# Three score banks, two first-pass banks, and a half unit made ahead of the context matmuls

## What is computed

```python
x = x + attn(layernorm(x))
    # content = einsum('bqhd,bkhd->bhqk', q + u_bias, k)
    # pos     = rel_shift(einsum('bqhd,khd->bhqk', q + v_bias, p))
    # attn    = softmax((content + pos) / sqrt(128));  ctx = attn @ v @ Wo
x = x + ffn(layernorm(x))
    # router: Wr1, layernorm, gelu, Wr2, softmax, top 2
    # y = (x1 * gelu(x2)) @ W2[e], weighted and added for the two experts
```

## Time and profile before

| what | value |
|---|---|
| median of 3 runs | 1681.2 us (1679.35 to 1681.27) |
| the profiled execution | 1680.72 us |
| its span, first to last instruction | 1679.0 us |
| attention loop, in the span | 88 to 1234 us |
| expert phase, in the span | about 1310 us to the end |

### The profile page before, as it was taken

One profiled execution on the slowest core, in us unless ns is written; L12 is line 12 of the kernel. 1 busy time (PEld: TensorE's weight loads), 2 busy tenths in 40 slices (PEclk: granted clock), 3 DMA queues, 4 the chain that ended last, 5 costly groups with the idle time before them and its releaser, 6 DMA issues. The chain is left out here.

```text
span 1679.0 us, 50905 instructions
## 1 busy us (share of the span) xinstructions
PE 1548.0 (92%) x12492; PEld 1204.6 (72%) x12493; DVE 1397.8 (83%) x5262; ACT 1108.9 (66%) x2295; POOL 1103.0 (66%) x2088
## 2 busy tenths in 40 slices
PE   3789999999999999999999999999952699999997
PEld 1567776677777767777777776776741699999997
DVE  4669899989989987998998899899864588887886
ACT  2157777776777776677777777767730477777775
POOL 5247767767766775777677677667673276666665
PEclk8679999999999998999999999999985799999999
DMA  5746535535644553464365355346454244444443
GB/s 136 198 116 174 148 93 152 164 96 128 180 116 128 161 148 84 110 203 110 104 174 148 93 141 164 97 129 179 122 153 136 42 58 54 56 56 52 56 53 49
DMA packets 133844, 199.72 MB, mean 119 GB/s; under 512 B 20888, under 2 KB 95016, under 8 KB 133632
## 3 DMA queue, kind: packets, MB, share of 16 engines
q1 hardware_dynamic: 108064, 177.07, 39.0%
q0 software_dynamic: 25568, 20.14, 8.2%
HBM read 108.10 MB, written 75.20 MB: 109 GB/s over the span
## 5 line engine op out<-in xcount | busy, mean ns | idle before, releaser
L1084 DVE CUSTOM_DVE_ANT_0 junk<-pA,lmask 128x512 bf16<-128x512 f32 x1056 | 686.9, 683 | 65.1 <-PE pA L671 45.9
L986 ACT ACTIVATE prob<-pB 128x512 f32<-128x512 f32 x384 | 229.8, 598 | 205.5 <-PE pB L690 115.9
L1578 POOL DMA_INDIRECT out<-yb,dst x142 | 230.4, 1622 | 131.3 <-ACT yb L1656 78.5
L692 PE MATMUL pB<-QL,K 97*128 97x512 f32 (+3 forms) x768 | 286.4, 373 | 1.4 <-ACT upper_diag L986 1.2
L669 PE MATMUL pA<-K,QL 96*128 96x512 f32 (+3 forms) x792 | 282.1, 357 | 5.1 <-DMA K<-split_operands 3.4
L690 PE MATMUL pB<-QU,K 97*128 97x512 f32 (+3 forms) x640 | 267.5, 418 | 0.2
L671 PE MATMUL pA<-K,QU 96*128 96x512 f32 (+3 forms) x660 | 233.1, 354 | 4.4 <-DVE acc L1084 3.2
L988 ACT ACTIVATE prob<-pB 128x512 f32<-128x512 f32 x384 | 227.9, 594 | 12.7 <-PE pB L692 3.4
L708 PE MATMUL pC<-prob,vext 128*17 128x256 f32 x3088 | 217.8, 385 | 0.1
L576 POOL TENSOR_TENSOR prob<-prob,upper_diag 128x128 f32<-128x128 f32 x384 | 179.7, 468 | 31.9
L690 PEld LDWEIGHTS pB<-QU,K 97*128 97x128 f32 x640 | 122.0, 191 | 99.9 <-issue 62.3
(11 more groups left out here) (305 smaller groups left out, 3642.9 us busy)
## 6 DMA issues: line engine op xcount, KB each, us to landing
QL<-split_operands SPq DMA_DIRECT2D x67, 256.0 KB
QU<-split_operands SPq DMA_DIRECT2D x67, 256.0 KB
K<-split_operands SPq DMA_DIRECT2D x67, 256.0 KB
xg<-routed_rows SPq DMA_DIRECT2D x75, 132.0 KB
split_operands<-c_h SPq DMA_DIRECT2D x36, 256.0 KB, 6.1
split_operands<-c_l SPq DMA_DIRECT2D x36, 256.0 KB, 6.4
QL<-split_operands SPq DMA_DIRECT2D x67, 128.0 KB
QU<-split_operands SPq DMA_DIRECT2D x67, 128.0 KB
```

What stands on the lines that cost most here:

```text
L692: mm = pe.matmul(pB[:, q0 + up:q0 + HALF], K[0:r, s, k], QL[0:r, s, q0 + up:q0 + HALF], start=True, stop=True)
L986: act.activation(p[:, 0:HALF], pB[:, 0:HALF], ACT.Exp, scale=SCALE).then_inc(p_exp, 1)
L1084: v.tensor_tensor_reduce(out, src[:, :], lmask[:, at:at + HALF], 1.0, -3.0e38, ALU.add, ALU.max, acc[:, s, qb, n % 2:n % 2 + 1]).then_inc( ...
L1578: po.indirect_dma_start(dram["out"], bass.IndirectOffsetOnAxis(dst[k][:, a:a + 1], 0), yb[k][:, a, :], None, compute_op=ALU.add).then_inc( ...
```

## The change

`pB` becomes three tensors of one bank each (`S2_BUFS = 3`), and `S1_BUFS` goes from 3 to 2. Half units are counted through, g = 2 x unit + half, and half g goes into `pB[g % 3]`; it waits until the exponential of half g-3 has been taken. A chunk waits until VectorE has read chunk n-2. At the places where contexts follow a unit (u = 1, 4, 6, 8), the first half of the next unit is issued before the contexts and no longer after them and the small work. Before and after the loop the third extra bank is `pB[2]` and no longer `pA[2]`. Line numbers shift by 2 to 6.

```diff
-S1_BUFS = 3
+S1_BUFS = 2
+S2_BUFS = 3
...
-        pB, pC = pb("pB", [P, S]), pb("pC", [P, S // STRIPS])
+        pB, pC = [pb(f"pB{i}", [P, HALF]) for i in range(S2_BUFS)], pb("pC", [P, S // STRIPS])
+        outside = (*pA, pB[2])
...
             def project(nb, j, part=0, parts=1):
-                dst = (pE, *pA)[j % 4] if first else pE
+                dst = (pE, *outside)[j % 4] if first else pE
...
             def second_pass(b, h, u, half):
-                pe.wait_ge(p_exp, HPB * (b * (H * S2U) + h * S2U + u) + half + 1)
-                r, q0 = MROW + 1, HALF * half
+                g = HPB * (h * S2U + u) + half
+                pe.wait_ge(p_exp, HPB * (b * (H * S2U)) + max(g, 1))
+                r, q0, dst = MROW + 1, HALF * half, pB[g % S2_BUFS]
...
-                        mm = pe.matmul(pB[:, q0:q0 + up], K[0:r, s, k], QU[0:r, s, q0:q0 + up], start=True, stop=True)
+                        mm = pe.matmul(dst[:, 0:up], K[0:r, s, k], QU[0:r, s, q0:q0 + up], start=True, stop=True)
...
                     for u in range(S2U):
-                        second_pass(b, h, u, 0)
+                        if (h, u) == (0, 0) or (u - 1) % S2U not in PAIRS_AT:
+                            second_pass(b, h, u, 0)
                         first_pass(b, h + AHEAD, 2 * u)
                         second_pass(b, h, u, 1)
                         first_pass(b, h + AHEAD, 2 * u + 1)
                         if u in PAIRS_AT:
+                            if (h, u) != (H - 1, S2U - 1):
+                                second_pass(b, h + (u + 1) // S2U, (u + 1) % S2U, 0)
                             back, kb = PAIRS_AT[u]
                             context(b, h + back, kb)
...
             pe.wait_ge(s1_read, (B * H + AHEAD) * S1U)
+            pe.wait_ge(p_exp, HPB * (B * H * S2U + 1))
             for j in range(2):
                 pe.wait_ge(m_done, m_at(B, f"turn {j}") + 1)
-                project_out(j, pA[1 + j]).then_inc(w_ready, 1)
-            pe.wait_ge(p_exp, HPB * (B * H * S2U + 1))
+                project_out(j, outside[1 + j]).then_inc(w_ready, 1)
...
-                        act.activation(p[:, 0:HALF], pB[:, 0:HALF], ACT.Exp, scale=SCALE).then_inc(p_exp, 1)
+                        act.activation(p[:, 0:HALF], pB[HPB * n % S2_BUFS][:, :], ACT.Exp, scale=SCALE).then_inc(p_exp, 1)
                         act.wait_ge(s2_ready, HPB * (b * (H * S2U) + n) + 3)
-                        act.activation(p[:, HALF:S], pB[:, HALF:S], ACT.Exp, scale=SCALE).then_inc(p_exp, 1)
+                        act.activation(p[:, HALF:S], pB[(HPB * n + 1) % S2_BUFS][:, :], ACT.Exp, scale=SCALE).then_inc(p_exp, 1)
```

More of the change, by code:

```diff
@@ L689, in second_pass @@
                     if up > 0:
-                        mm = pe.matmul(pB[:, q0:q0 + up], K[0:r, s, k], QU[0:r, s, q0:q0 + up], start=True, stop=True)
+                        mm = pe.matmul(dst[:, 0:up], K[0:r, s, k], QU[0:r, s, q0:q0 + up], start=True, stop=True)
                     if up < HALF:
-                        mm = pe.matmul(pB[:, q0 + up:q0 + HALF], K[0:r, s, k], QL[0:r, s, q0 + up:q0 + HALF], start=True, stop=True)
+                        mm = pe.matmul(dst[:, up:HALF], K[0:r, s, k], QL[0:r, s, q0 + up:q0 + HALF], start=True, stop=True)
                 else:
@@ L695, in second_pass @@
                         k = slice(k0, k0 + P)
-                        mm = pe.matmul(pB[:, k], K[0:r, s, k], QU[0:r, s, k], start=True, stop=True)
+                        mm = pe.matmul(dst[:, k0 - q0:k0 - q0 + P], K[0:r, s, k], QU[0:r, s, k], start=True, stop=True)
                 mm.then_inc(s2_ready, 1)
@@ L870, in _ @@
             pe.wait_ge(m_done, m_at(B, "rows 1") + 1)
[L871 to L874, removed]
+            router_hidden(range(NB), outside[1]).then_inc(m_ready, 1)
+            router_fold(B, outside[2]).then_inc(m_ready, 1)
+            router_logits(B, pB[0]).then_inc(m_ready, 1)
+            router_ranks(B, pB[1]).then_inc(m_ready, 1)
         @block.scalar
@@ L887, in evacuate @@
                 half = slice(HALF * (j % 2), HALF * (j % 2) + HALF)
-                src = (pE, *pA)[j % 4] if isinstance(nb, int) and nb == 0 else pE
+                src = (pE, *outside)[j % 4] if isinstance(nb, int) and nb == 0 else pE
                 if j < 2:
@@ L1037, in _ @@
                 copied(f"rows {j}", (pE, pA[0])[j], m_done)
-            fold(B, pA[2])
+            fold(B, outside[2])
             tanh(B)
@@ L1370, in _ @@
                 v.wait_ge(w_ready, B * W_N + 1 + j)
-                final(j, pA[1 + j], w_done)
+                final(j, outside[1 + j], w_done)
                 router_stats(B, range(4 * j, 4 * j + 4))
@@ L1375, in _ @@
             v.wait_ge(m_ready, m_at(B, "hidden") + 1)
-            router_bias(B, pA[1])
+            router_bias(B, outside[1])
             hidden_stats(B)
@@ L1382, in _ @@
             v.wait_ge(m_ready, m_at(B, "logits") + 1)
-            logits_out(pB[:, 0:HALF])
+            logits_out(pB[0])
             for part in range(4):
@@ L1386, in _ @@
             v.wait_ge(m_ready, m_at(B, "ranks") + 1)
-            places(B, 0, pB[:, HALF:S])
+            places(B, 0, pB[1])
             for part in (1, 2):
```

## The result

The changed kernel takes 1728.0 us (median; 1726.7 to 1732.3) against 1681.2 us (a fourth run of the kernel before took 1690.4 and leaves that median as it is): ratio 1.027, interval 1.023 to 1.031. It is slower by 47 us; 40 were forecast (1721, range 1698 to 1746).

The account below looks back on a forecast made before the run. TensorE was taken to bound the loop through its start-to-start times. From the profiled 1680.7 us, 40 - 2.6 - 1 + 0 + 4 = +40.4 gave 1721 us, range 1698 to 1746.

Parts of the forecast that it names:

- Part 1: Attention loop: chunks wait longer with two chunk banks, 40 us in eight turns, less 2.6 for a vanished router-row wait.
- the six places: Loop, (head step, unit): (0, 8), (1, 4), (2, 1), (3, 3), (4, 3), (4, 8), with delays of 0.31 to 0.97 us.
- (1, 4): Head step 1, unit 4 of the loop: chunk delayed 0.87 us, of which 0.19 vanishes in an existing wait, leaving 0.68.
- (5, 1): Head step 5, unit 1: a further 0.3 us delay, left out because TensorE waits behind it for VectorE's router work anyway.
- Part 2: Attention loop: three score banks shorten TensorE's waits for exponentials, a gain of 1 us, ends 0 and 8.
- Part 3: Attention loop: issuing the next unit's first half ahead of the contexts is worth 0, with 2 us either way.
- Part 4: Outside the loop: 34 chunks ahead of it cost 1 to 7 us more with two banks, taken as +4 us.
- What would show it: Signs in the trace after: turn 146 to 147 us, VectorE idle 5 us more, head steps 2 and 3 lengthened most.
- a sign against the bank wait: Loop: the bank wait is not the cause if head steps 1 to 4 do not lengthen more than 5 to 7.
- The clock: Rival: more TensorE waiting puts three or four more loop turns at the low clock, to 1750 us; chance 0.14.
- Absorbed: Rival: TensorE has slack in the loop that makes up part of the 5 us a turn, 1683 to 1706; chance 0.14.
- Faster: Rival: the score bank was the loop's true shortage, so the gain passes the cost, 1666 us; chance 0.06.

Follow-up runs that it names:

- the run with six waits: Kernel before, with only the chunks at (0, 8), (1, 4), (2, 1), (3, 3), (4, 3) and (4, 8) in the loop waiting for chunk n-2: 1703.6 us, ratio 1.014.

## Why the prediction was right, and where it was not

**What bounds the kernel.** TensorE, through its start-to-start times: right. One wait more for every chunk lengthens the turn by 4.9 us with nothing else changed. The rule on the busy share of weight loads (the Trainium skill, "Perfetto Trace Analysis", Identifying the Most-Contended Engine) would have had TensorE at 71% with slack to absorb it. The weight loads' share still reads 69% (100.8 of 146.26), and the loss was paid almost in full. The measurement decides for start-to-start times here.

**Part 1, 40 us less 2.6.** The loop lost 37.6. The delays at the six places are right to 0.02 us each when they stand alone, and the sum is right by errors that cancel, which is luck. In the run with the wait in the loop alone, the steps up add to 6.3 us a turn and the steps down to 1.6. The prediction had about 5.2 and 0.5.

The steps up. The six places, each with the chunks that lead up to it, give 3.6 us there and not 4.1: at (1, 4) the step is 0.40 and not 0.87, because TensorE comes there already 0.64 us late from the waits before and VectorE 0.18. The prediction had let each run of chunks start afresh. All other places together give 2.7 us and not 1.1: 0.59 at (7, 6), and about 0.1 us at each of fourteen more, some just behind a named one ((2, 2), (4, 4)).

The steps down. But for (1, 4), the prediction looked for swallowing waits only among rows in which TensorE itself is called idle. The largest one, 0.54 us at (1, 1), has 0.17 us in such a row; the rest hides in the modelled end of a matmul and shows only in starts: 0.82 us apart (685.83 and 686.65) where 0.42 is enough, and 0.44 (685.39 and 685.83) where 0.29 is. The one at (3, 6) is 0.48 to 0.49 and not 0.33 for the same reason. In the kernel before:

```profile
730.55 0.39 PE L669 MATMUL pA<-K,QL 96*128 96x512 f32 x1
731.22 0.66 PE L749 MATMUL pM<-ident_f,rows_r 128*128 128x128 f32 x4 [0.28 <-DVE rows_r L1159]
```

0.67 us from start to start where the run with six waits has 0.24, and 0.28 of it in the row of idle time. What the prediction left out at (5, 1) was rightly left out for the most part: 0.25 us are given back at (5, 4).

**Part 2, 1 us, ends 0 and 8.** Right: the third score bank in the old order is worth 0.1 us a turn, at most 0.2, so 1 to 2 us in all.

**Part 3, 0.** Right as a sum (146.23 and 146.26 us), incomplete as a reason. The prediction said that nothing on TensorE is late for want of exponentials except as in part 2. That holds only with the third bank: with two banks the same order costs 3.4 us a turn with three chunk banks, 1.6 with two. The step that was missed is that an instruction placed ahead of contexts stops them too if it waits.

**Part 4, 4 us.** The term that was mis-sized. The wait costs 6.8 us where the clock is low throughout, and the two profiles differ by 9.0 because the clock of that stretch, which varies between executions, adds 3.3 and an earlier first chunk takes off 1.0. The price of 0.2 us a chunk at the low clock was right (6.8 us over 34 chunks is 0.20); that half of the chunks run at full clock was not: in the profile after none does, and in the one before a third of the stretch did.

**What would show it.** The turn was put at 146 to 147 us: 146.26. VectorE idle 5 us more: 3.7, with 1.1 more busy. By the last read-outs of each, head steps 0 to 7 grew by 0.7, 0.4, 1.2, 0.3, 0.4, 0.7, 0.3 and 0.9 us. Step 2 grew most and step 6 little, as said, but step 3 grew by 0.3 and not 0.8, and steps 5 and 7 by more than 1, 3 and 4, which comes close to what the prediction had called a sign against the bank wait. The run with the wait in the loop alone settles it: nothing but chunk waits differs there, and the steps grow by the same numbers to 0.1 us (0.7, 0.4, 1.2, 0.3, 0.5, 0.8, 0.3, 0.9). It was the map of places that was off: most of the delay at (3, 3) is given back within step 3, the one at (4, 8) is read out in step 5 (which grew by 0.5 us in the run with six waits too, with none of them in it), and step 7 has (7, 6), which was on the list.

**The rivals.** The clock made no difference in the loop (one long and one short low stretch before and after, and the loop's first 13 us, which the prediction did not count among them; 0.99), and took part only ahead of it. The part of the Trainium skill on banks and the clock ("TensorE: Matmul & The Clock Gate", A second HAM failure mode: psum-queue depth-cycling) has no case here: with waits at every chunk bank the turns stay at 1.00. "Absorbed" took a quarter of the loss (1.6 of 6.3 us a turn), too little to decide. "Faster" fell with the table above. (What it took from the Trainium skill on gaps that repeat stands in "Perfetto Trace Analysis", Optimization Strategy, and not in the section named.)

## What to carry to other kernels

A bank is worth what its queue's waits would cost, and these can be read before anything is built: for each instruction, the end of the reader that one bank less would make it wait for, against its start now. Before moving a bank from one queue to another, try the stricter wait in the old code; it prices the bank in one run. And put ahead of independent work only what does not have to wait there, since in an engine's order a waiting instruction holds everything behind it.

## What the runs showed of the hardware

The stretch from the first chunk to the loop runs at a granted clock of 0.50 to 0.67 from one execution to another with the same instructions and waits (six profiles), and its length goes from 33.0 to 29.6 us with it. The loop is entered at the low clock in every profile and leaves it 12 to 24 us later; the first turn takes 7 to 12 us more than the others.

Later in the loop the clock falls to its lower level one to four times in an execution (27 times in the eleven profiles), each time in head step 6, but in different turns. In the two profiles of before and after, long falls cost 6.2 us and short ones 1.6. By their cost they can make much of the spread between medians of one kernel; turns at full clock repeat to 0.2 us or better. In the kernel before, the two falls (at 633.6 and 923.7) come just behind eight matmuls of 8 columns (L637, from 632.62 and 921.89), in a place that all eight turns have; why two of eight fall is not shown.

A bank is handed over in 0.05 to 0.07 us: that long after VectorE's read-out or ScalarE's exponential ends, TensorE's waiting matmul starts.
